# Gated cross-attention stack on one core: GpSimd in place of VectorE for the gate's normalised rows of ten batches

## The chip, the core and the metric

The kernel runs on one core of a Trainium2 chip, as one program with one launch. Its time is the device time of that core in microseconds. Three runs of the kernel before gave 856.76, 857.04 and 859.95 us; the median, 857.04 us, is what the forecast is set against.

The core has four compute engines with a queue of instructions each: TensorE (PE in the profile: matrix products and transposes), VectorE (DVE), ScalarE (ACT) and GpSimd (POOL). SyncE (SP) starts DMAs. Engines wait for each other through semaphores only; each engine works its queue strictly in the order in which the code wrote it.

## The reference

A stack of four gated layers on `x` (8 batches of 256 rows of width 256), with a context of 8 x 120 rows. Each layer is a cross-attention and a feed-forward part, both on normalised rows and both added through `tanh` of a gate:

```python
x = x + jnp.tanh(g_xattn[0]) * _L0_xattn_ref(_layernorm(x, axis=-1), ctx_1024, ctx_1024, ...)
x = x + jnp.tanh(g_ffn[0]) * _L0_ffn_ref(_layernorm(x, axis=-1), L0_ffn_gate, ...)
...
x = x + jnp.tanh(g_xattn[3]) * _L3_xattn_ref(ctx_1024, ctx_1024, _layernorm(x, axis=-1), ...)
x = x + jnp.tanh(g_ffn[3]) * _L3_ffn_ref(_layernorm(x, axis=-1), L3_ffn_wg, L3_ffn_w1, L3_ffn_w2)
```

with

```python
def _layernorm(x, axis=-1, eps=1e-05):
    m = jnp.mean(x, axis=axis, keepdims=True)
    v = jnp.var(x, axis=axis, keepdims=True)
    return (x - m) / jnp.sqrt(v + eps)
```

The first layer (0) and the last (3) have an attention with one head and a feed-forward part with experts. In both the experts' gate is a product of the normalised rows with a 256 x 8 matrix: in layer 0 each expert takes its 256 best tokens (`top_k` over the softmax) and a shared hidden layer works on all tokens; in layer 3 each token goes to its best expert, up to a capacity of 256. Layers 1 and 2 have attention with 16 heads, a spectral and a ternary feed-forward part; the change doesn't touch them.

## The kernel before, in words

All of `x` stays in SBUF, as 16 tiles of 128 rows x 256, two tiles a batch. The program goes: weights folded; **layer 0's attention and gate**, batch by batch (about 15 to 80 us); the shared hidden layer with the search for each expert's tokens beside it; the first experts; the two many-head layers as one stream; **layer 3's attention and gate** (about 670 to 740 us); the last experts.

The two bold stages are the same code, `one_gate(L)`, written once for each engine, with `L` 0 or 3. Each is a loop over steps `s`. A step works on several batches at once: the attention of batch `s` begins, the attention of batch `s-1` ends, and the gate of batch `s-2` is computed. Nothing but the order of the calls in each engine's loop sets the order of the work. The order of one step `s`:

- VectorE: `stats(one, s+1, 0)`, the mean and variance of the next batch for its attention (`bn_stats` L1745, `bn_aggr` L1748, plus epsilon L1750); `normalize(gt, s-2, 1, z2)`, the **gate's normalised rows** (L1760, two instructions, one a tile); `shift(s)`, the scores' maximum (L1773); `take_logits(s-3)` (L1791); `normalize(one, s+1, 0, z)`, the attention's normalised rows (L1760 too); `add_output(s-1)` (L1778, L1780, and L1784, which adds the attention's product to `x`); `take_values(s+1)` (L1768); `stats(gt, s-1, 1)`, the statistics for the gate, of rows that now hold the attention's result. In layer 3 there is routing work between these from step 5 on (L1801 to L1836).
- GpSimd: `rstd_of(one, s+1, 0)`, variance to the power -0.5 for the attention of the next batch (L456), then `rstd_of(gt, s-1, 1)`, the same for the gate. From step 7 of layer 3 it also starts the DMAs that move routed rows (L448).
- TensorE: `turn_z(s)` (transposes, L772), `turn_p(s-1)` (L802), `keys_values(s+1)`, `scores(s)`, `gate_turn(s-2)`, the **transposes of the gate's rows** (L823), then `values(s-1)`, the attention's product that `add_output` waits for, and `logits(s-2)`. All products have the line of the helper `mm`, L676. Before some of the transposes there are products without use (`FILL`: six before the first gate batch of layer 0, six before the sixth of layer 3).
- ScalarE copies transposes out of PSUM (L1414) and does the exponentials (L1466).
- SP stores the gate's rows of layer 0 to DRAM (L333), each after the semaphore `gate_z`, because the experts gather them from there later. In its queue the loads of the shared layer's weights (L338) stand behind the fourth of these stores.

The gate's rows go to `z2` in layer 0 (four tiles, used in turn) and to `zx` in layer 3 (a place for every tile). In the profile both are parts of one SBUF buffer, `arena`; the statistics and the powers lie in `small`. The semaphores by their names in the order of instructions: `one_var`, `one_rstd`, `one_z`, `one_y_ps` for the attention, `gate_var`, `gate_rstd`, `gate_z`, `gate_zT_ps` for the gate: statistics made, power made, rows made, and (`zT_ps`) rows transposed; `gate_stored0` and `gate_stored1` count landed stores; `one_y_ps` is the product in `values`.

Of the kernel before, what the change touches and what calls it, by code (L numbers as in the profile page):

```python
# [5 lines left out]
ALU = mybir.AluOpType  # L6
# [8 lines left out]
D = 256  # L15
KC = D // P
NB, SQ, SK = 8, 256, 120
T = NB * SQ
NT = T // P
TB = SQ // P  # L20
# [8 lines left out]
FILL = {0: {0: 6}, 3: {5: 6}}  # L29
GROUPS = [(0, 3), (3, 5), (5, 7), (7, 8)]  # L30
EARLY = 2 * GROUPS[0][1]
EPS = 1e-5
NEG = -1e30
BITS = 32
# [23 lines left out]
def flamingo_kernel(nc, d, out):  # L58
    ctx = ExitStack()
    with ctx:  # L60
# [7 lines left out]
        x = sb("x", [P, NT, D], F32)  # L68
# [52 lines left out]
        z = c.take(4 * D, "p (t n) -> p t n", t=4)  # L121
        zT = c.take(2 * KC * SQ, "p (u k n) -> p u k n", u=2, k=KC)
        z2 = c.take(4 * D, "p (t n) -> p t n", t=4)
# [54 lines left out]
        zx = c.take(NT * XROW, "p (t n) -> p t n", t=NT)  # L178
# [9 lines left out]
        c.at = after_common + 2 * KC * CAP + 2 * MC * CAP + 2 * TB * D  # L188
        late = c.take((NT - 2 - EARLY) * CAP, "p (i n) -> p i n", i=NT - 2 - EARLY)
        assert c.at <= 14272  # L190
# [38 lines left out]
        mv = c.take(8, "p (t n) -> p t n", t=4)  # L229
        ve = c.take(4)  # L230
        rstd = c.take(4)
# [63 lines left out]
        gt = sems("gate", f"{ln_names} l_ps l_sb stored0 stored1 picked prob rank_ps rank_sb slot moved")  # L295
# [139 lines left out]
        def _(g):  # L435
# [15 lines left out]
            def one_gate(L):  # L451
                b0 = NB * (L // 3)

                def rstd_of(q, k, a):
                    g.wait_ge(q["var"], b0 + k + 1)
                    g.tensor_tensor(rstd[:, 2 * a:2 * a + 2], ve[:, 2 * a:2 * a + 2], mhalf[:, 0:2], ALU.pow).then_inc(q["rstd"], 1)  # L456

                if L == 0:
                    rstd_of(one, 0, 0)
                for s in range(NB + 1):  # L460
                    if s + 1 < NB:
                        rstd_of(one, s + 1, 0)
                    if L == 3 and s in (7, 8):
                        if s == 7:
                            g.wait_ge(ex["blank"], 16)
                            g.wait_ge(gt["slot"], 1)
                        for t in range(3 * (s - 7), 3 * (s - 6)):
                            move(t)
                    if 1 <= s:
                        rstd_of(gt, s - 1, 1)  # L470
                if L == 3:
                    g.wait_ge(ex["rows0"], 16)
                    for n, (a, b) in enumerate(GROUPS[1:]):
                        g.wait_ge(gt["slot"], 5 if b == NB else n + 2)
                        for t in range(2 * a, 2 * b):
                            move(t)
# [1250 lines left out]
        def _(v):  # L1727
# [12 lines left out]
            def one_gate(L):  # L1740
                b0 = NB * (L // 3)
# [69 lines left out]
                def take_ranks(n):  # L1811
                    w = 2 * (GROUPS[n][1] - GROUPS[n][0])
                    o = psum[4][:, 256:256 + w * E].rearrange("p (t e) -> p t e", t=w)
                    v.wait_ge(gt["rank_ps"], n + 1)
                    V.tensor_scalar(o8[:, 0:w, :], o, float(CAP), float(2 * T), ALU.is_gt, ALU.mult)
                    V.tensor_tensor(a8[:, 0:w, :], o, bcast(base8, 1, w), ALU.add).then_inc(gt["rank_sb"], 1)
# [27 lines left out]
                def main():  # L1844
# [19 lines left out]
                    for s in range(NB + 3):  # L1864
# [4 lines left out]
                        if L == 3 and s == NB + 1:  # L1869
                            take_logits(s - 3)  # L1870
                            pick_expert(2)
                        if 2 <= s < NB + 2:
                            normalize(gt, s - 2, 1, z2)
                        if s < NB and (L or s):
                            shift(s)
# [14 lines left out]
                            take_values(s + 1)  # L1890
                        if L == 3 and s == 6:
                            take_ranks(0)
                        if 1 <= s <= NB:
                            stats(gt, s - 1, 1)
                        if L == 3 and s == 6:
# [224 lines left out]
            def stream():  # L2120
# [69 lines left out]
                def side_stats(j):  # L2190
# [6 lines left out]
                    v.drain()  # L2197
                    V.tensor_scalar(veS, mv[:, 2:4, 1], EPS, None, ALU.add).then_inc(f1["var"], 1)

# [193 lines left out]
```

## Time and profile before

| | us |
|---|---|
| median of three runs | 857.04 |
| the three runs | 856.76, 857.04, 859.95 |
| span of the profiled execution | 859.9 |
| time of that execution (the run that stands for it) | 859.95 |
| TensorE busy | 829.8 (96% of the span), clock granted 0.993 of 2.4 GHz on average |
| VectorE busy | 459.7 (53%) |
| ScalarE busy | 332.7 (39%) |
| GpSimd busy | 227.6 (26%) |

How to read it: a share of the span is a mean over stages that are limited in different ways. The two stages of `one_gate` together last about 125 us; VectorE is busy for 80 to 90% of most of that time, and for almost nothing in the expert stages. The span and the time of the profiled execution differ by less than 0.1 us, so what lies around the span can be left out of account.

### The profile page before, as it was taken

What the parts mean: (1) busy time and instruction counts of PE and PEld (TensorE: products, weight loads), DVE (VectorE), ACT (ScalarE), POOL (GpSimd) and SP (SyncE); (2) the same over time, 40 slices, a digit from 0 to 9 for tenths busy, and PEclk for the clock granted to TensorE, in tenths of its full rate; (3) what the DMA queues carried; (4) which work ended last, traced back from release to release, by engine and by line L of the source; (5) the groups of instructions that cost most, each with busy time, mean ns of one, the idle gap of its engine ahead of it and who ended that gap; (6) DMA issues with size and microseconds to landing.
All of it is one profiled execution on the core that took longest, in us unless ns stands there. A gap on an engine that the chain in (4) does not pass through costs nothing.

```text
span 859.9 us, 15359 instructions
## 1 busy us (share of the span) xinstructions
PE 829.8 (96%) x5870; PEld 645.0 (75%) x5870; DVE 459.7 (53%) x1245; ACT 332.7 (39%) x642; POOL 227.6 (26%) x304
## 2 busy tenths in 40 slices
PE   8999999999999998899999999988999998999996
PEld 7875665678888886667777777755777777888885
DVE  3773775500132318677777777764999787100000
ACT  3344112112313224556455545646554444321211
POOL 1211333020425221001001301213788124421212
PEclk9998999999999999999999999999999999999999
DMA  7141911015746439000000000000000012454541
GB/s 247 26 147 41 351 29 52 26 44 208 238 134 229 117 79 339 2 2 2 2 1 2 2 2 2 2 1 2 1 1 2 26 38 87 149 191 140 188 138 23
DMA packets 35427, 71.14 MB, mean 83 GB/s; under 512 B 10642, under 2 KB 25370, under 8 KB 30491
## 3 DMA queue, kind: packets, MB, share of 16 engines
q1 hardware_dynamic: 28489, 60.46, 19.8%
q0 software_dynamic: 6144, 8.31, 5.0%
q10 hardware_dynamic: 722, 1.39, 0.4%
q8 instruction: 47, 0.77, 0.4%
q14 instruction: 25, 0.20, 0.1%
HBM read 55.50 MB, written 14.80 MB: 82 GB/s over the span
## 4 chain that ended last, share of the span: by engine, by line
PE 84%; DVE 8%; DVEq 2%; issue 2%; ACT 1%; DMA 1%; POOL 1%; POOLq 0%; SPq 0%; ACTq 0%
PE banks L676 76%; DVE small L2166 2%; PE banks L1223 2%; PE banks L1305 1%; PE banks L823 1%; PE banks L1237 1%; PE banks L1040 1%; ACT arena L1632 1%; DVE arena L1760 1%; PE banks L1261 1%; PE banks L1114 1%; DVEq L2167 0%; DVE small L1745 0%; PE banks L772 0%; DMA x<-acc 0%
## 5 line engine op out<-in xcount | busy, mean ns | idle before, releaser
L676 PE MATMUL banks<-arena 32*120 32x256 f32 (+6 forms) x1848 | 167.5, 375 | 7.4 <-DVE small L2166 4.2
L1414 ACT ACTIVATE arena<-banks 128x512 f32<-128x512 f32 (+4 forms) x183 | 105.7, 597 | 156.9 <-PE banks L823 34.1
L676 PEld LDWEIGHTS banks<-arena 32*120 32x120 f32 (+5 forms) x1848 | 105.6, 162 | 37.7 <-issue 16.1
L676 PE MATMUL banks<-ffw,arena 128*128 128x256 f32 (+2 forms) x640 | 117.3, 338 | 0.2 <-DVE x L1738 0.2
L676 PE MATMUL banks<-arena,ew 128*128 128x256 f32 x512 | 113.2, 380 | 0.7 <-ACT arena L1414 0.7
L676 PE MATMUL banks<-ew,arena 128*128 128x256 f32 x512 | 113.3, 380 | 0.0
L676 PEld LDWEIGHTS banks<-arena,ew 128*128 128x128 f32 x512 | 97.4, 190 | 14.1 <-ACT arena L1414 1.1
L676 PEld LDWEIGHTS banks<-ew,arena 128*128 128x128 f32 x512 | 96.4, 190 | 12.3
L676 PEld LDWEIGHTS banks<-ffw,arena 128*128 128x128 f16 (+1 forms) x640 | 84.5, 135 | 24.3 <-issue 3.0
L2166 DVE TENSOR_REDUCE small<-banks 128x16 f32<-128x1920 f32 x32 | 69.0, 2157 | 19.1 <-PE banks L676 18.9
L1632 ACT ACTIVATE arena<-banks,mcol 120x2048 f32<-120x2048 f32 x32 | 63.1, 1973 | 16.2 <-PE banks L676 16.2
L2113 DVE TENSOR_SCALAR arena<-banks,arena 128x256 f32<-128x256 f32 x16 | 7.1, 480 | 110.3 <-PE banks L676 110.3
L578 POOL TENSOR_TENSOR small<-small,mhalf 128x2 f32<-128x2 f32 x16 | 11.1, 692 | 195.6 <-DVE small L2137 195.6
L676 PE MATMUL banks<-arena,ffw 128*128 128x512 f32 x128 | 60.2, 615 | 0.0
L1573 ACT ACTIVATE arena<-banks,b1T 128x256 f32<-128x256 f32 x64 | 26.8, 470 | 77.0 <-PE banks L676 77.0
L1444 ACT ACTIVATE arena<-banks,b1T 128x512 f32<-128x512 f32 x32 | 21.9, 687 | 76.9 <-PE banks L676 76.9
L1575 ACT ACTIVATE arena<-banks 128x256 f32<-128x256 f32 x64 | 21.1, 381 | 78.1 <-PE banks L676 78.1
L456 POOL TENSOR_TENSOR small<-small,mhalf 128x2 f32<-128x2 f32 x31 | 22.6, 730 | 95.8 <-DVE small L1750 95.8
L2082 DVE TENSOR_SCALAR small<-arena,tg 128x2 f32<-128x2 f32 x8 | 1.8, 228 | 82.6 <-PE banks L676 82.6
L543 POOL DMA_INDIRECT arena<-zrow,small x16 | 17.8, 1114 | 101.4 <-DVE arena L2095 55.0
L533 POOL DMA_INDIRECT out<-arena x14 | 21.8, 1559 | 80.4 <-DVE arena L2113 64.8
L596 POOL TENSOR_TENSOR arena<-arena 128x256 f32<-128x256 f32 x64 | 38.8, 638 | 10.0 <-ACT arena L1659 9.9
(258 smaller groups left out, 1252.5 us busy)
## 6 DMA issues: line engine op xcount, KB each, us to landing
ew<-in_w SPq DMA_DIRECT2D x32, 1024.0 KB, 7.2
xrow<-arena SPq DMA_DIRECT2D x1, 2064.0 KB, 22.1
zrow<-arena SPq DMA_DIRECT2D x8, 256.0 KB, 2.2
ffw<-in_shared SPq DMA_DIRECT2D x2, 1024.0 KB, 6.9
acc<-x SPq DMA_DIRECT2D x4, 512.0 KB, 3.6
ffw<-in_tern SPq DMA_DIRECT2D x2, 1024.0 KB, 7.9
out<-x SPq DMA_DIRECT2D x8, 256.0 KB, 2.0
arena<-xrow SPq DMA_DIRECT2D x7, 258.0 KB, 4.1
```

Of the source, the lines that this page charges most:

```text
L456: g.tensor_tensor(rstd[:, 2 * a:2 * a + 2], ve[:, 2 * a:2 * a + 2], mhalf[:, 0:2], ALU.pow).then_inc(q["rstd"], 1)
L533: g.indirect_dma_start(to, bass.IndirectOffsetOnAxis(ap=at(e, j), axis=0), eout[:, e % 2, j, :], None, compute_op=ALU.add, **kw).then_inc( ...
L543: g.indirect_dma_start(G[:, u, j, 0:ROW], None, zrow, bass.IndirectOffsetOnAxis(ap=idx[:, TB * e + j:TB * e + j + 1], axis=0))\
L596: m = g.tensor_tensor(hw[:, t % 2, a:a + 256], h2[:, t % 2, a:a + 256], wrow[:, a:a + 256], ALU.mult)
L676: return pe.matmul(o, l, r, start=a, stop=b)
L1223: m = pe.transpose(OW[:, 512 * t + g_ * P:512 * t + (g_ + 1) * P], OP[:, g_, t * P:(t + 1) * P], ident[:, :])
L1414: return nc.scalar.activation(o, i_, ACT.Copy)
L1444: nc.scalar.activation(hT[:, m_, :], psum[m_ % 4][:, :], ACT.Gelu_apprx_tanh, bias=b1T[:, E * MC + m_:E * MC + m_ + 1]).then_inc(sh["h_sb" ...
L1573: m = nc.scalar.activation(heT[:, u, m_, :], src, ACT.Gelu_apprx_tanh, bias=b1T[:, n * MC + m_:n * MC + m_ + 1])
L1575: m = nc.scalar.activation(heT[:, u, m_, :], src, ACT.Relu)
L1632: nc.scalar.activation(PT[0:SK, c].rearrange("p h n -> p (h n)"), SC[0:SK, :], ACT.Exp, bias=mcol[0:SK, L - 1, k:k + 1]).then_inc(q["p_exp ...
L2166: V.tensor_reduce(nmx[:, t, :], s, AX.X, ALU.max, negate=True).then_inc(q["max"], 1)
```

## The change

GpSimd computes the gate's normalised rows for the first six batches of layer 0 and the first four of layer 3; VectorE does the rest as before. The new function `gate_rows(k)` stands in GpSimd's loop between the two powers of a step. It waits for GpSimd's own earlier instructions (`drain`), in layer 0 from the third batch on also for the transposes and the store that free its tiles, and raises the same semaphore as before. VectorE, which overwrites the mean and the statistics of the gate with the next batch's, now waits for that semaphore before it does so.

```diff
@@ -29,6 +29,7 @@
 EARLY = 2 * GROUPS[0][1]
+POOLED = {0: 6, 3: 4}
@@ -455,11 +456,25 @@
+                def gate_rows(k):
+
+                    g.drain()
+                    if k >= 2 and L == 0:
+                        g.wait_ge(gt["zT_ps"], k - 1)
+                        g.wait_ge(gt[f"stored{k % 2}"], 16 * (k // 2))
+                    for t in range(TB):
+                        dst = zx[:, 2 * k + t, 0:D] if L == 3 else z2[:, 2 * (k % 2) + t, :]
+                        m = g.tensor_scalar(dst, x[:, 2 * k + t, :], mv[:, 2 + t, 0:1], rstd[:, 2 + t:3 + t],
+                                            ALU.subtract, ALU.mult)
+                    m.then_inc(gt["z"], 1)
+
                 if L == 0:
                     rstd_of(one, 0, 0)
                 for s in range(NB + 1):
                     if s + 1 < NB:
                         rstd_of(one, s + 1, 0)
+                    if 2 <= s < 2 + POOLED[L]:
+                        gate_rows(s - 2)
@@ -1869,7 +1884,7 @@
-                        if 2 <= s < NB + 2:
+                        if 2 + POOLED[L] <= s < NB + 2:
                             normalize(gt, s - 2, 1, z2)
@@ -1890,6 +1905,8 @@
+                        if 2 <= s <= 1 + POOLED[L]:
+                            v.wait_ge(gt["z"], b0 + s - 1)
                         if 1 <= s <= NB:
                             stats(gt, s - 1, 1)
```

GpSimd's instructions in layer 0, from the first gate batch on, before the change:

```order
L456 TENSOR_TENSOR small<-small,mhalf 128x2 [waits gate_var]
L456 TENSOR_TENSOR small<-small,mhalf 128x2 [waits one_var]
L456 TENSOR_TENSOR small<-small,mhalf 128x2 [waits gate_var]
L456 TENSOR_TENSOR small<-small,mhalf 128x2 [waits one_var]
L456 TENSOR_TENSOR small<-small,mhalf 128x2 [waits gate_var]
```

and the same stretch of the changed program (its lines are numbered some 15 higher):

```order
L457 TENSOR_TENSOR small<-small,mhalf 128x2 [waits gate_var]
L457 TENSOR_TENSOR small<-small,mhalf 128x2 [waits one_var]
L467 TENSOR_SCALAR arena<-x,small 128x256 x2
L457 TENSOR_TENSOR small<-small,mhalf 128x2 [waits gate_var]
L457 TENSOR_TENSOR small<-small,mhalf 128x2 [waits one_var]
L467 TENSOR_SCALAR arena<-x,small 128x256 x2
L457 TENSOR_TENSOR small<-small,mhalf 128x2 [waits gate_var]
```

Each pair of row instructions stands behind the power that waits for the attention's statistics of the next batch, and in front of the next power for the gate.

VectorE's instructions of step 3 in layer 0, from the next batch's statistics on, before the change:

```order
L1745 BN_STATS small<-x 128x6 x2
L1748 BN_AGGR small<-small 128x2 x2
L1750 TENSOR_SCALAR small<-small 128x2
L1760 TENSOR_SCALAR arena<-x,small 128x256 [waits gate_rstd]
L1760 TENSOR_SCALAR arena<-x,small 128x256
L1773 TENSOR_REDUCE small<-banks 128x2 [waits one_s_ps]
L1791 COPY small<-banks 128x16 [waits gate_l_ps]
L1760 TENSOR_SCALAR arena<-x,small 128x256 [waits one_zT_ps,one_rstd]
L1760 TENSOR_SCALAR arena<-x,small 128x256
```

and in the changed program, up to the gate's statistics:

```order
L1760 BN_STATS small<-x 128x6 x2
L1763 BN_AGGR small<-small 128x2 x2
L1765 TENSOR_SCALAR small<-small 128x2
L1788 TENSOR_REDUCE small<-banks 128x2 [waits one_s_ps]
L1806 COPY small<-banks 128x16 [waits gate_l_ps]
L1775 TENSOR_SCALAR arena<-x,small 128x256 [waits one_zT_ps,one_rstd]
L1775 TENSOR_SCALAR arena<-x,small 128x256
L1793 RECIPROCAL small<-small 128x2 [waits one_p_sb]
L1795 TENSOR_SCALAR small<-small,tg 128x2
L1799 SCALAR_TENSOR_TENSOR x<-banks,small,x 128x256 [waits one_y_ps]
L1799 SCALAR_TENSOR_TENSOR x<-banks,small,x 128x256
L1783 TENSOR_TENSOR arena<-banks,rows 120x256 [waits one_y_ps,one_KT_sb]
L1760 BN_STATS small<-x 128x6 [waits gate_z]
```

The gate's pair is gone from between the statistics and the maximum; the statistics for the gate wait for `gate_z`. TensorE's and SP's instructions and their waits are the same in both.

## Rows read from the trace of the kernel before

**Rows 1.** The page's chain that ended last, by engine, over the whole span.
```profile
PE 84%; DVE 8%; DVEq 2%; issue 2%; ACT 1%; DMA 1%; POOL 1%; POOLq 0%; SPq 0%; ACTq 0%
```

**Rows 2.** TensorE's waits, whole span: total us, times, longest us.
```profile
PE banks L823 <- DVE arena L1760: 4.2, 6, 1.6
```

**Rows 3.** Timeline, TensorE, first layer: start us, us, instructions, [idle before <- releaser].
```profile
30.12 0.60 PE L823 MATMUL banks<-ident,arena 128*128 128x128 f32 x4
...
43.05 0.63 PE L823 MATMUL banks<-ident,arena 128*128 128x128 f32 x4
...
49.40 0.60 PE L823 MATMUL banks<-ident,arena 128*128 128x128 f32 x4
...
55.95 0.63 PE L823 MATMUL banks<-ident,arena 128*128 128x128 f32 x4
...
61.89 1.04 PE L823 MATMUL banks<-ident,arena 128*128 128x128 f32 x4 [0.62 <-DVE arena L1760]
...
68.99 3.47 PE L676 MATMUL banks<-arena,ffw 128*128 128x512 f32 x4
```

**Rows 4.** Timeline, VectorE, first layer.
```profile
44.62 0.88 DVE L1784 SCALAR_TENSOR_TENSOR x<-banks,small,x 128x256 f32<-128x256 f32 x2
...
47.21 0.74 DVE L1745 BATCH_NORM_STATS2 small<-x 128x6 f32<-128x256 f32 x2
...
48.49 0.73 DVE L1760 TENSOR_SCALAR arena<-x,small 128x256 f32<-128x256 f32 x2
...
64.67 0.88 DVE L1784 SCALAR_TENSOR_TENSOR x<-banks,small,x 128x256 f32<-128x256 f32 x2 [2.16 <-PE banks L676]
...
72.33 0.94 DVE L1760 TENSOR_SCALAR arena<-x,small 128x256 f32<-128x256 f32 x2 [0.80 <-POOL small L456]
```

**Rows 5.** Timeline, GpSimd, first layer.
```profile
29.40 0.78 POOL L456 TENSOR_TENSOR small<-small,mhalf 128x2 f32<-128x2 f32 x1 [0.91 <-DVE small L1750]
...
48.60 0.85 POOL L456 TENSOR_TENSOR small<-small,mhalf 128x2 f32<-128x2 f32 x1 [0.53 <-DVE small L1750]
...
60.28 0.69 POOL L456 TENSOR_TENSOR small<-small,mhalf 128x2 f32<-128x2 f32 x1 [4.26 <-DVE small L1750]
...
72.62 0.97 POOL L483 TENSOR_SCALAR rows<-rows,tg 128x256 f32<-128x256 f32 x1
```

**Rows 6.** Timeline, TensorE, last layer: the gate's transposes of batches 1, 4 and 5.
```profile
683.25 0.66 PE L823 MATMUL banks<-ident,arena 128*128 128x128 f32 x4 [1.09 <-DVE arena L1760]
...
701.99 0.63 PE L823 MATMUL banks<-ident,arena 128*128 128x128 f32 x4
...
709.68 0.63 PE L823 MATMUL banks<-ident,arena 128*128 128x128 f32 x4 [1.57 <-DVE arena L1760]
```

**Rows 7.** Timeline, GpSimd, two instructions with a drain between them.
```profile
663.94 0.22 POOL L601 TENSOR_SCALAR small<-small 128x1 f32<-128x1 f32 x1
664.31 0.56 POOL L603 TENSOR_TENSOR small<-small,mhalf 128x1 f32<-128x1 f32 x1
```

**Rows 8.** Groups by line and shape, GpSimd: busy us, mean ns, idle before.
```profile
L508 POOL TENSOR_SCALAR rows<-rows,tg 128x256 f32<-128x256 f32 x3 | 2.8, 936 | 4.0 <-DVE small L1945 4.0
...
L513 POOL TENSOR_SCALAR arena<-arena 8x120 f32<-8x120 uint8 x1 | 0.6, 622 | 0.1
```

**Rows 9.** Timeline, GpSimd, last layer: power for the attention's fourth batch.
```profile
682.63 0.78 POOL L456 TENSOR_TENSOR small<-small,mhalf 128x2 f32<-128x2 f32 x1 [0.53 <-DVE small L1750]
```

**Rows 10.** Timeline, SP's queue, first layer: the loads of the shared weights.
```profile
49.66 0.95 SPq L338 DMA_DIRECT2D ffw<-in_shared  x2
```

**Rows 11.** Windows: us, PE, PEld, DVE, ACT, POOL busy (x), PEclk, DMA share, GB/s.
```profile
60.00:62.00 2.00, 1.38 (x10) 1.11 (x10) 1.16 (x5) 0.00 (x0) 0.69 (x1) 0.99 0.00 0
62.00:64.00 2.00, 2.00 (x7) 1.73 (x7) 0.44 (x4) 1.03 (x4) 0.00 (x0) 0.50 0.38 131
...
72.00:74.00 2.00, 2.00 (x8) 1.01 (x7) 0.94 (x2) 1.04 (x2) 1.59 (x3) 0.95 0.00 0
...
708.00:710.00 2.00, 0.43 (x5) 0.35 (x4) 1.85 (x10) 0.00 (x0) 0.78 (x1) 1.00 0.00 0
```

## The prediction

> **What bounds the kernel now.** I read the chain of waits first, then TensorE's waits, then the two stages that the change touches, engine by engine. The chain lies on TensorE for 84% of the span and on VectorE for 8% [rows 1], so anything that keeps TensorE waiting is paid in full, and anything that only relieves VectorE is paid back only where TensorE waits for it. TensorE's own list says where that is: before the gate's transposes (L823) it waits for the normalised rows (L1760) six times, 4.2 us in all [rows 2]. That 4.2 us is the most that faster rows could give.
>
> In the first layer the gate's transposes follow each other evenly: the first is at 30.12, the fifth at 55.95, so a step takes 25.83 / 4 = 6.46 us, and none of these has a wait in front [rows 3]. A step is one loop of four links. (a) From the gate's transposes, TensorE's product and VectorE's addition (L1784) start 44.62 - 43.05 = 1.57 us later. (b) VectorE then does the addition, takes the values, makes the gate's statistics and comes to the next batch's statistics at 47.21: 2.59 us later [rows 3, 4]. (c) GpSimd starts the power (L456) on those at 48.60, 1.39 us later [rows 5]. (d) VectorE meanwhile writes the gate's rows at 48.49, in 0.73 us [rows 4], and the next transposes go at once. In the last layer the same loop takes (701.99 - 683.25) / 3 = 6.25 us [rows 6].
>
> **The change, part by part.** VectorE loses ten pairs of L1760, 0.73 us each, 7.3 us in all. I cost this relief at nothing: in the loop above the pair is replaced by something longer, and the relief behind it only makes VectorE wait earlier for the product that comes after the gate's transposes. The wait for the rows that VectorE gets before the gate's statistics costs nothing either, because those stand behind the addition, which already waits for a product that TensorE makes after it has turned the rows.
>
> The rows move to GpSimd, and the order of GpSimd's instructions decides when they come: the power for the attention's next batch stands in front of them. They can't start when the statistics of the gate are ready, but only after (c). So a step's rows now need, from the start of that power:
> - the power, 0.69 us: it takes 0.78 and 0.85 where VectorE's pair runs beside it and 0.69 where it doesn't [rows 5], and that pair is gone;
> - the drain, 0.15 us: a GpSimd instruction that ends at 663.94 + 0.22 has its successor behind a drain at 664.31 [rows 7];
> - the two instructions. No row of before has this form (128x256, two operations, both with a column of scalars). The nearest below is the same shape with one operation, 936 ns [rows 8] (the single one at 72.62 took 0.97 [rows 5]). The nearest above has two operations on 120 elements, 622 ns [rows 8], which scaled by 256/120 is 1.33 us. I take 1.0, near the same shape, since the upper one contains a fixed part and a conversion from bytes. The pair is 2.0 us, with ends 1.87 and 2.65;
> - 0.18 us from the rows to the transposes, as between VectorE's rows (48.49 + 0.73) and the transposes at 49.40 [rows 3, 4].
>
> Together 3.02 us from the power's start. Link by link the loop becomes 1.57 + 2.59 + 1.39 + 3.02 = 8.57 us.
>
> First layer, six batches. The first batch: its power starts at 29.40 [rows 5], rows are usable at 32.42 where TensorE began at 30.12: +2.3. Four loops: 4 x (8.57 - 6.46) = +8.4. The sixth batch has no attention batch in front of it: the power of its own statistics starts at 60.28 [rows 5], 4.33 us after the fifth transposes (55.95), and 4.33 + 3.02 = 7.35 replaces 61.89 - 55.95 = 5.94 [rows 3]: +1.4. Sum +12.1 us.
>
> Last layer, four batches. The first: 682.63 [rows 9] + 3.02 = 685.65 against 683.25 [rows 6]: +2.4. Three loops: 3 x (8.57 - 6.25) = +7.0. The fifth batch is written by VectorE again, and its chain from the fourth transposes, 709.68 - 701.99, is VectorE's [rows 6]: no change. Sum +9.4 us.
>
> The stores of the gate's rows wait on the same semaphore and move with them. SP's queue has the load of the shared weights behind the fourth store: it goes out at 49.66 [rows 10]; and no DMA is busy any more from 60 us on [rows 11], so it takes 10 us at most. It would go some 8.6 us later (2.3 + 3 x 2.11) and be there by 69; TensorE uses it first at 68.99 + 12.1 = 81.1 [rows 3]. Hidden, with 12 us to spare. The wait for that store before the third and later batches asks for one two steps back, two loops of 6.46 us and more earlier. Also hidden.
>
> So far +21.5 us with TensorE at its full clock. The clock is the second term. The granted clock went from 1.00 (2.4 GHz) to 0.50 (1.2 GHz) at 62 us, after a stretch in which TensorE had been busy 1.38 of 2 us, and was back by 72 to 74 us [rows 11]. In the last layer it stayed at 1.00 through a stretch with 0.43 of 2 us busy [rows 11], with a wait of 1.57 us in front of the transposes [rows 6]. Idle spells that are now 0.6 to 1.6 us long and rare become about 2.1 us in every step, longer than any that these rows show. At the low clock link (a) took 64.67 - 61.89 = 2.78 instead of 1.57 us [rows 3, 4]: +1.21 in each step whose transposes fall into it; the rest of TensorE's work has the step's slack. I count it for five steps of the first layer, where a smaller spell was enough, and two of the last: 7 x 1.21 = +8.5 us. Bounds: none, or all of TensorE's work (below).
>
> Sum: 12.1 + 9.4 + 8.5 = **+30.0 us**. The profiled execution spans 859.9 us and is the highest of the three runs; against the median of 857.04 the forecast is **887.0 us**.
>
> On GpSimd's neighbours: beside a GpSimd multiplication, VectorE's pair took 0.94 instead of 0.73 us [rows 4, 5]; a power beside it took up to 0.85 instead of 0.69. So the two slow each other by 0.1 to 0.2 us, and I add nothing. The Trainium skill (SBUF — State Buffer, section "Who interferes with whom") says more: such VectorE instructions and GpSimd share a pair of ports, held by one for its whole instruction while the other is fully blocked. The sum by it is the second rival's. The rows at 72.33 and 72.62 speak against it: VectorE's second instruction ended at 73.27, inside GpSimd's 72.62 to 73.59.
>
> **The rivals.**
> - *The clock holds.* No idle spell of the last layer lowered it [rows 6, 11]. Then 857.0 + 21.5 = 878.5 us; with the pair at its ends (10 x -0.13, 10 x +0.65) 877 to 885. 27%.
> - *The rows are held up by VectorE.* GpSimd's pair now runs beside VectorE's remaining pair for the attention (0.73 us) in nine of ten steps (the sixth batch has none). If one fully stops the other, the rows come up to 0.73 later: +6.6 on the forecast, 893.6 us. For it: the power's 0.85 beside the pair, against it 72.33. The port rule above is this case. 10%.
> - *The clock stays low through both stages.* TensorE's own step is then what lasts: 6.46 x 2.78 / 1.57 = 11.4 instead of 8.57, eight times, on top of 878.5: +23, 901 us. Against it: it was back ten us after the fall. 8%.
> - *GpSimd is as fast as VectorE* on this form: the pair 0.73 instead of 2.0, 1.27 less in ten batches, and with less waiting the clock holds: 878.5 - 12.7 = 866 us. Its rows of 936 ns for one operation speak against it. 7%.
> - *Not slower:* the freed VectorE gives TensorE its waits back. The place is the last layer, where VectorE is level with TensorE; the prize is a part of the 4.2 us [rows 2], so 855 to 857 us. It decides by one point: the rows must be usable within 2.19 us of the start of VectorE's statistics, as at present (49.40 - 47.21 [rows 3, 4]). GpSimd's power alone ends at 1.39 + 0.69 = 2.08. It would take rows that get in front of that power, and GpSimd's order has them behind it. That the change wouldn't do what it says can be excluded in the same way: the order shows ten pairs on GpSimd. 4%.
>
> **How the numbers follow.** The forecast, 44%: 887.0, its own range 880 to 894 (three to ten steps at the low clock, and the pair's upper end). The range is 869 to 899: it leaves out the last two rivals and the low clock throughout, 19%, and takes in the rest. 0.5% of this kernel is 4.3 us, about what a measurement can tell from no change. Slower by more: all but the last rival, 95%, as even the fast-GpSimd case is 8 us up. Same 3%, faster 2%.
>
> **What would show it.** In the profile after: ten pairs of TENSOR_SCALAR 128x256 on GpSimd, about 1.0 us each, starting 0.8 to 0.9 us after the power's start; L823's waits now released by GpSimd, near 2 us in each of ten steps, some 20 us in all; transposes 8.5 us apart in both layers (9.7 where the clock is low); GpSimd some 20 us busier, VectorE 7.3 us less; more stretches at a granted clock of 0.5 before 80 us and around 685 to 715 us; everything between the stages just shifted by some 12 to 18 us. Wrong it is if the transposes stay 6.5 us apart, if the GpSimd pair takes well under 1.8 us, or if the distance from the power to the rows shows a start that isn't behind it.

## The result: 38 us slower, and the profile after

The changed kernel took 896.59 us in the median of four runs (893.86 to 899.76), the kernel before 858.50 us (856.76 to 861.50, four runs). The ratio is 1.0454, with a 95% interval of 1.0432 to 1.0475: slower by 38.1 us. The forecast was 887.0 us with a range of 869 to 899, so the sign and the place were right, and 9.6 us of the time were missed. The measured time lies above the 880 to 894 that the forecast gave to its own mechanism, near the upper end of the range.

Two things about the reference point. The kernel before runs in two ways: in one set of seven runs four took 856.67 to 856.86 us, at a mean clock of 0.997 to 0.999, and three took 861.56 to 861.80 at 0.992 to 0.993. And the time of a run is 1.7 to 2.1 us more than its span, in every run whose span is listed (861.74 with a span of 860.0; 893.86 with 891.8). The profiled execution of before, with its span of 859.9, was thus one of those at 861.7 us, 4.7 above the median, and not the one of 859.95 us as the table ahead of the prediction had it. The 4.9 us between the two ways fit the stretch at low clock after 62 us [rows 11]. No profile of a better execution of before is at hand, but e3 below has the same first layer without that stretch, and it is 4.8 us shorter. Below, "clean before" is the kernel before without that stretch (856.86 us).

The first lines of the page of the changed kernel, the row of the granted clock in 40 slices (22.3 us each), and the chain by engine:

```profile
span 891.8 us, 15369 instructions
...
PE 846.4 (95%) x5870; PEld 659.2 (74%) x5870; DVE 453.9 (51%) x1225; ACT 333.0 (37%) x642; POOL 252.6 (28%) x324
...
PEclk9876999999999999999999999999999779999999
...
PE 81%; DVE 8%; POOL 3%; DVEq 3%; issue 2%; ACT 2%; POOLq 1%; ACTq 0%
```

GpSimd is on the chain with 3% of the span, 27 us, where it had 1% [rows 1]. VectorE is 5.8 us less busy and gained nothing by it. The granted clock is below full in five slices, three of the first layer and two of the last. TensorE is "busier" by 16.6 us with the same 5870 instructions: no new work, but more of it at 1.2 instead of 2.4 GHz.

TensorE's waits in front of the gate's transposes (L823 before, L838 now):

```profile
PE banks L838 <- POOL arena L467: 16.0, 6, 4.2
...
PE banks L838 <- DVE arena L1775: 2.5, 3, 1.9
```

Six waits of 16.0 us for GpSimd stand where six of 4.2 us for VectorE stood [rows 2]; the four other steps with GpSimd's rows have none. The transposes themselves show why. They are, in the first layer and the last (start, time for four; the wait is in brackets), with the first large product of the shared layer and the transposes of the seventh batch (88.23):

```profile
32.44 0.80 PE L838 MATMUL banks<-ident,arena 128*128 128x128 f32 x4 [2.78 <-POOL arena L467]
...
42.42 0.63 PE L838 MATMUL banks<-ident,arena 128*128 128x128 f32 x4 [0.24 <-POOL arena L467]
...
51.49 0.63 PE L838 MATMUL banks<-ident,arena 128*128 128x128 f32 x4 [2.55 <-POOL arena L467]
...
61.91 1.06 PE L838 MATMUL banks<-ident,arena 128*128 128x128 f32 x4
...
71.90 1.09 PE L838 MATMUL banks<-ident,arena 128*128 128x128 f32 x4 [2.79 <-POOL arena L467]
...
81.11 1.09 PE L838 MATMUL banks<-ident,arena 128*128 128x128 f32 x4
...
86.52 1.88 PE L691 MATMUL banks<-arena,ffw 128*128 128x512 f32 x4
88.23 0.60 PE L838 MATMUL banks<-ident,arena 128*128 128x128 f32 x4
...
703.40 1.12 PE L838 MATMUL banks<-ident,arena 128*128 128x128 f32 x4 [4.15 <-POOL arena L467]
...
713.70 0.63 PE L838 MATMUL banks<-ident,arena 128*128 128x128 f32 x4
...
723.27 1.09 PE L838 MATMUL banks<-ident,arena 128*128 128x128 f32 x4 [3.45 <-POOL arena L467]
...
733.57 0.60 PE L838 MATMUL banks<-ident,arena 128*128 128x128 f32 x4
...
741.52 0.63 PE L838 MATMUL banks<-ident,arena 128*128 128x128 f32 x4 [1.85 <-DVE arena L1775]
```

The first four steps of the first layer take 9.98, 9.07, 10.42 and 9.99 us, where a step took 6.46, and the sixth batch comes 9.21 us after the fifth instead of 5.94 [rows 3]. In the last layer the steps take 10.30, 9.57 and 10.30, where they took 6.25 [rows 6]. The seventh batch's transposes came at 72.30 in before's profile; they are 15.9 us later now.

**One loop at full clock** is the second step, 42.42 to 51.49. GpSimd and VectorE in it:

```profile
38.97 0.69 POOL L457 TENSOR_TENSOR small<-small,mhalf 128x2 f32<-128x2 f32 x1 [0.49 <-DVE small L1765]
39.85 2.43 POOL L467 TENSOR_SCALAR arena<-x,small 128x256 f32<-128x256 f32 x2 [0.19 <-issue]
46.73 0.71 POOL L457 TENSOR_TENSOR small<-small,mhalf 128x2 f32<-128x2 f32 x1 [4.45 <-DVE small L1765]
47.94 0.69 POOL L457 TENSOR_TENSOR small<-small,mhalf 128x2 f32<-128x2 f32 x1 [0.50 <-DVE small L1765]
48.89 2.46 POOL L467 TENSOR_SCALAR arena<-x,small 128x256 f32<-128x256 f32 x2 [0.26 <-issue]
```

```profile
43.96 0.88 DVE L1799 SCALAR_TENSOR_TENSOR x<-banks,small,x 128x256 f32<-128x256 f32 x2 [0.22 <-PE banks L691]
...
49.38 0.88 DVE L1775 TENSOR_SCALAR arena<-x,small 128x256 f32<-128x256 f32 x2
```

The power at 46.73 is the gate's own; the rows could start 0.7 us later. They wait for the one at 47.94, the attention's, which VectorE's statistics release. Link by link: transposes at 42.42, addition at 43.96 (1.54 later; forecast 1.57), the attention's power at 47.94 (3.98; forecast 2.59 + 1.39 = 3.98), the power 0.69 (0.69), the drain 0.26 (0.15), the pair 2.46 (2.0), and 0.14 from 51.35 to the transposes at 51.49 (0.18). Every link but two is as forecast to 0.04 us. The loop is 9.07 instead of 8.57.

**Loops at low clock.** Two-microsecond windows of all engines (stretch, its length, then busy time of PE, PEld, DVE, ACT and POOL in us, granted clock as a share of 2.4 GHz, DMA share, GB/s):

```profile
40.00:42.00 2.00, 2.00 (x13) 1.35 (x11) 0.00 (x0) 0.61 (x2) 2.00 (x2) 1.00 0.02 4
...
58.00:60.00 2.00, 2.00 (x5) 0.80 (x3) 0.00 (x0) 0.61 (x2) 2.00 (x2) 0.50 0.00 0
60.00:62.00 2.00, 2.00 (x10) 1.94 (x10) 0.00 (x0) 0.00 (x0) 0.38 (x1) 0.50 0.35 118
...
720.00:722.00 2.00, 0.00 (x0) 0.00 (x0) 1.30 (x6) 0.00 (x0) 1.81 (x3) 1.00 0.00 0
...
724.00:726.00 2.00, 2.00 (x8) 1.64 (x6) 0.00 (x0) 1.28 (x5) 0.00 (x0) 0.50 0.00 0
```

TensorE stands idle while the rows are made (720 to 722 us: busy 0.00 us, clock still 1.00), and is at 1.2 GHz afterwards (724 to 726: 0.50) through the work of the step. It is back 6 to 13 us after the fall. It falls five times in the ten steps, about every second step: in or just behind each of the five waits of 2.55 to 4.15 us for GpSimd above, and not at the other five transposes, which had a wait of 0.24 us or none. At low clock the work of a step fills it: GpSimd's pair ended at 60.38, but the transposes came at 61.91, with no wait, since TensorE was still at work. That step took 10.42 us, and its bound was TensorE.

### The profile page after: what moved, and what is told of

It reads as the page before. It is cut to its first block, busy times and chain, and to the rows that moved or that the text cites. A ratio compares the mean times of both kernels' runs of the same rounds, so it can differ in the third digit from the quotient of the medians.

```text
span 891.8 us, 15369 instructions
## 1 busy us (share of the span) xinstructions
PE 846.4 (95%) x5870; PEld 659.2 (74%) x5870; DVE 453.9 (51%) x1225; ACT 333.0 (37%) x642; POOL 252.6 (28%) x324
## 3 DMA queue, kind: packets, MB, share of 16 engines
q10 hardware_dynamic: 722, 1.39, 0.4%
## 4 chain that ended last, share of the span: by engine, by line
PE 81%; DVE 8%; POOL 3%; DVEq 3%; issue 2%; ACT 2%; POOLq 1%; ACTq 0%
PE banks L691 74%; DVE small L2183 2%; POOL arena L467 2%; PE banks L1238 2%; PE banks L838 1%; PE banks L1320 1%; PE banks L1252 1%; PE banks L1055 1%; ACT arena L1647 1%; PE banks L1276 1%; PE banks L1129 1%; POOL small L457 1%; DVE arena L1775 1%; DVE x L1799 1%; DVE small L1760 0%
## 5 line engine op out<-in xcount | busy, mean ns | idle before, releaser
L691 PE MATMUL banks<-arena 32*120 32x256 f32 (+6 forms) x1848 | 172.3, 378 | 7.4 <-DVE small L2183 4.1
L691 PEld LDWEIGHTS banks<-arena 32*120 32x120 f32 (+5 forms) x1848 | 109.1, 164 | 38.8 <-issue 16.6
L2183 DVE TENSOR_REDUCE small<-banks 128x16 f32<-128x1920 f32 x32 | 69.0, 2157 | 18.5 <-PE banks L691 18.3
L611 POOL TENSOR_TENSOR arena<-arena 128x256 f32<-128x256 f32 x64 | 39.0, 642 | 10.7 <-ACT arena L1674 10.5
```

The source lines that it names most:

```text
L611: m = g.tensor_tensor(hw[:, t % 2, a:a + 256], h2[:, t % 2, a:a + 256], wrow[:, a:a + 256], ALU.mult)
L691: return pe.matmul(o, l, r, start=a, stop=b)
L2183: V.tensor_reduce(nmx[:, t, :], s, AX.X, ALU.max, negate=True).then_inc(q["max"], 1)
```

## The experiments

Every experiment has its own runs of the kernel before, on the same chip as it. In the first set (e1 to e4) they have a median of 856.86 us over seven runs, in the last (e5) 856.93 over eleven. A set between (e7 to e10) was on a chip where the kernel before takes 866.34 us in the median of 29 runs; it is compared by ratios within the set, and by distances in the traces.

### e1: the clock held with products without use

```diff
-FILL = {0: {0: 6}, 3: {5: 6}}
+FILL = {0: {0: 16, 1: 10, 2: 10, 3: 10, 4: 10, 5: 8}, 3: {0: 14, 1: 10, 2: 10, 3: 10, 5: 6}}
```

> The changed kernel with products without use in front of the gate's transposes of the ten batches (8 to 16 of them, 0.225 us each at the full clock), so that TensorE works through most of its wait; nothing else differs. Theory A (the rows come late by GpSimd's chain, and the low clock is a second term): the granted clock stays at 1.0 in both stages, the transposes are 9.0 us apart in both layers (1.57 + 2.59 + 1.39 + 0.69 + 0.20 + 2.43 + 0.14), against 9.1 to 10.4 in the changed kernel, and the time falls by some 8 to 14 us to 883 to 889. Rival B (the low clock is only a sign of the waiting and costs nothing): the time stays at 896 within 3 us. Rival C (the products get in the way): slower than 896.

Measured 886.96 us (884.90 to 888.76), ratio 1.0325 [1.0276, 1.0373]; the changed kernel has 1.0454. The mean clock is 0.992 to 0.998 instead of 0.963 to 0.970. The gate's transposes in the first layer, with the seventh batch's, and two of the last layer:

```profile
32.38 0.66 PE L838 MATMUL banks<-ident,arena 128*128 128x128 f32 x4 [0.55 <-POOL arena L467]
...
41.36 0.65 PE L838 MATMUL banks<-ident,arena 128*128 128x128 f32 x4
...
68.36 0.66 PE L838 MATMUL banks<-ident,arena 128*128 128x128 f32 x4 [0.22 <-POOL arena L467]
...
76.21 0.66 PE L838 MATMUL banks<-ident,arena 128*128 128x128 f32 x4 [0.71 <-POOL arena L467]
...
82.04 0.60 PE L838 MATMUL banks<-ident,arena 128*128 128x128 f32 x4
...
732.31 0.98 PE L838 MATMUL banks<-ident,arena 128*128 128x128 f32 x4 [1.57 <-DVE arena L1775]
...
742.99 0.60 PE L838 MATMUL banks<-ident,arena 128*128 128x128 f32 x4
```

The steps of the first layer are all 9.0 us long ((68.36 - 32.38) / 4), the pure loop. The clock's share of the loss is 896.59 - 886.96 = 9.6 us between medians, and 11.6 us against the two runs of 884.9 and 885.2 that kept the clock nearly throughout. In the profiled run it still fell behind the wait of 1.57 us at 732.31, and the next transposes came 10.68 us later, where 7.0 is usual [rows 6]: that is the 3.7 us between its kinds of runs. What is left, 28 us, is the longer loop, and 1.2 us between the two stages that are counted below. Rivals B (the low clock costs nothing, 896 us) and C (the products get in the way) are thus wrong.

### e2 and e3: one layer at a time

```diff
-POOLED = {0: 6, 3: 4}
+POOLED = {0: 6, 3: 0}
```

> GpSimd makes the rows in the first layer alone (six batches, none in the last). The two traces give the first layer 16 to 17 us of the loss. Theory A: the parts add up, so 858.5 + 17 = 875 us, 873 to 879. Rival (one stage's delay moves or hides the other, by the clock or by a transfer): the two single-layer runs do not add up to the 38 us of the change.

and `{0: 0, 3: 4}`:

> GpSimd makes the rows in the last layer alone (four batches). The two traces give the last layer 14 to 15 us. Theory A: 858.5 + 15 to 20 = 873 to 879 us, and with the first-layer run the gains over before add up to 38 within 4 us. Rival as there.

Measured: the first layer alone 883.63 us (875.12 to 884.16), ratio 1.0261 [1.0194, 1.0328]; the last alone 870.91 (869.19 to 872.12), ratio 1.0144 [1.0099, 1.0189]. Against 856.86 these are +26.8 and +14.1, together +40.8, where the whole change makes +39.7 against the same 856.86 (+38.1 against the 858.50 of its own runs of before). The two add up, within their intervals; neither pays for or hides the other. Each alone missed what I expected of it: the first layer costs more (873 to 879 us expected), the last less (873 to 879 us again, where the traces alone had given it 14 to 15 us). In the first, part of that is a stage at low clock that reached further (its first large product came at 90.37, against 86.52 with the whole change), and one of its four runs, at 875.12 and a clock of 0.986, did without.

The trace of e3 also gives what was missing in before's: a first layer on VectorE whose clock holds.

```profile
29.96 0.60 PE L838 MATMUL banks<-ident,arena 128*128 128x128 f32 x4
...
55.79 0.63 PE L838 MATMUL banks<-ident,arena 128*128 128x128 f32 x4
61.72 0.63 PE L838 MATMUL banks<-ident,arena 128*128 128x128 f32 x4 [0.62 <-DVE arena L1775]
...
67.52 0.60 PE L838 MATMUL banks<-ident,arena 128*128 128x128 f32 x4
```

The seventh batch stands at 67.52, 4.8 us before the 72.30 of before's profile. This is the "clean before" against which the first layer is counted below.

### e4: the rows ahead of the attention's power

```diff
                 for s in range(NB + 1):
-                    if s + 1 < NB:
-                        rstd_of(one, s + 1, 0)
                     if 2 <= s < 2 + POOLED[L]:
                         gate_rows(s - 2)
+                    if s + 1 < NB:
+                        rstd_of(one, s + 1, 0)
```

> The changed kernel with GpSimd's two calls in the other order: the gate's rows before the power for the attention's next batch. Theory A (each step's loop is as long as its links): the rows start 0.20 us after the gate's own power, the loop is 4.16 + 0.86 + 0.20 + 2.43 + 0.14 = 7.8 instead of 9.0 us at the full clock, still above the 6.46 and 6.25 of before: with waits of about 1.5 us and a clock that falls in some steps 873 to 883 us. Rival B (the place in GpSimd's queue is not what delays the rows; the duration alone is): no gain, 893 to 900. Rival C: the attention's rows, whose power now comes later, become the wait (L787 transposes), and it stays above 885.

Measured 887.87 us (886.37 to 890.66), ratio 1.0352 [1.0303, 1.0400]. Steps at full clock take 8.07 and 8.04 us instead of 9.07. But the clock still fell:

```profile
38.71 0.63 PE L838 MATMUL banks<-ident,arena 128*128 128x128 f32 x4 [1.47 <-POOL arena L467]
...
46.75 1.09 PE L838 MATMUL banks<-ident,arena 128*128 128x128 f32 x4 [1.53 <-POOL arena L467]
...
58.71 1.06 PE L838 MATMUL banks<-ident,arena 128*128 128x128 f32 x4
```

One step, 46.75 to 58.71, took 11.96 us. TensorE worked through almost all of it at 1.2 GHz (granted clock 0.50 in every window from 48 to 60 us), so TensorE itself was the bound there. The order is worth 896.59 - 887.87 = 8.7 us of the 38, less than I expected (873 to 883 us), and this run doesn't tell how much of it is loop and how much clock. It lies above 885 as in rival C, but not by C's mechanism: in front of the attention's transposes (L787) TensorE waits 0.8 us in three waits, exactly as in the changed kernel. What lengthens it is the clock.

### e5: the same, with the clock held

The edit of e4 and, fewer than in e1 since the loop is shorter,

```diff
-FILL = {0: {0: 6}, 3: {5: 6}}
+FILL = {0: {0: 11, 1: 6, 2: 6, 3: 6, 4: 6, 5: 8}, 3: {0: 10, 1: 6, 2: 6, 3: 6, 5: 6}}
```

> The rows are made ahead of the power, as in e4_rows_first, and TensorE's wait is covered with useless products, as in e1_fill, but with fewer of them, since the loop is shorter: only the length of the loop at full clock is left of the change. Theory A (the loop and the clock are two separate costs): the clock holds, the gate's transposes stand 8.05 us apart in the first layer (e4_rows_first had 8.04 to 8.07 where its clock was full, e1_fill 9.0) and about as much in the last, so the kernel lies about ten steps x 0.95 us = 9 to 10 us below e1_fill: a ratio of 1.020 to 1.024 to its own kernel before. Theory B (the 8.7 us that e4_rows_first gained came mainly from a clock that was low for less time): with the clock held in both, the order is worth 3 to 5 us: a ratio of 1.027 to 1.030. TensorE should wait under 3 us in all for GpSimd's rows.

Measured 876.44 us (875.62 to 879.48, six runs), ratio 1.0220 [1.0193, 1.0246]: 10.5 us below e1, as theory A has it, and outside the 1.027 to 1.030 of theory B. Loop and clock are two separate costs; TensorE waits 2.3 us in all for GpSimd. Inside the loop, from the transposes at 46.92 to those at 54.96:

```profile
46.83 0.71 POOL L457 TENSOR_TENSOR small<-small,mhalf 128x2 f32<-128x2 f32 x1
51.53 0.69 POOL L457 TENSOR_TENSOR small<-small,mhalf 128x2 f32<-128x2 f32 x1 [3.99 <-DVE small L1765]
52.48 2.42 POOL L467 TENSOR_SCALAR arena<-x,small 128x256 f32<-128x256 f32 x2 [0.25 <-issue]
```

```profile
47.58 0.73 DVE L1775 TENSOR_SCALAR arena<-x,small 128x256 f32<-128x256 f32 x2 [1.63 <-POOL small L457]
...
48.77 0.88 DVE L1799 SCALAR_TENSOR_TENSOR x<-banks,small,x 128x256 f32<-128x256 f32 x2
```

The rows now start behind the gate's own power (51.53), which saves the 1.2 us between the two powers. But the attention's power comes late in its turn (46.83, behind the pair), VectorE waits 1.63 us for it, and the addition begins 1.85 us after the transposes instead of 1.54. So 0.3 us are given back, and the loop is 8.04, not 7.8. Whichever of the two goes first on GpSimd, the other one's reader waits. The +19.5 us that remain are mainly the price of the duration: the pair takes 2.42 us where VectorE writes the same rows in 0.73, and ten times the 1.69 us between them are 16.9 us. The drain, the 0.3 us given back and what lies between the stages are in the rest; no run takes them apart.

### e10: GpSimd's instruction with one operation

e1's idea with a pair that subtracts the mean only: this kernel leaves out the multiplication of the gate's rows of the ten batches by the power, and with it the column of scalars that it reads, so its result is not the reference's. The products without use are 8 a step.

```diff
-                        m = g.tensor_scalar(dst, x[:, 2 * k + t, :], mv[:, 2 + t, 0:1], rstd[:, 2 + t:3 + t],
-                                            ALU.subtract, ALU.mult)
+                        m = g.tensor_scalar(dst, x[:, 2 * k + t, :], mv[:, 2 + t, 0:1], None, ALU.subtract)
```

> The run with products in front of the transposes (e1), with GpSimd's two instructions doing one operation instead of two: the rows are x minus the mean and are not multiplied by the power, so the gate works on rows that are not scaled; fewer products (8 instead of 10) fit the shorter wait. Theory A (the form's duration goes into every step in full): 2 x 0.94 instead of 2 x 1.22 us, transposes 8.4 instead of 9.0 us apart, ten batches x 0.56 = 5.6 us less than e1's 887: 881. Rival (GpSimd's time per instruction doesn't depend on the second operation, the 1.22 us come from its column of scalars or from VectorE's neighbourhood): transposes 9.0 us apart, 887.

Measured 886.54 us (885.97 to 888.33) on the slower chip, ratio 1.0228 [1.0181, 1.0275]. Here is the group of GpSimd's instructions, in the changed kernel and then in e10 (count, busy us, mean ns; the mean holds the pairs that VectorE slowed, so it is above the 1.22 us of an undisturbed one):

```profile
L467 POOL TENSOR_SCALAR arena<-x,small 128x256 f32<-128x256 f32 x20 | 25.4, 1276 | 2.2 <-issue 2.2
```

```profile
L467 POOL TENSOR_SCALAR arena<-x,small 128x256 f32<-128x256 f32 x20 | 18.9, 954 | 2.1 <-issue 2.1
```

and one pair of e10 in the order of time:

```profile
37.91 1.86 POOL L467 TENSOR_SCALAR arena<-x,small 128x256 f32<-128x256 f32 x2 [0.19 <-issue]
```

The pair is 1.86 instead of 2.43, and the gate's transposes of the first layer stand 8.4 us apart instead of 9.0, as theory A has it; the rival (9.0) is wrong. The second operation costs 0.29 us an instruction, and 0.6 us of each loop. Ten loops make 6 us of it. Whether the operation itself costs this or the second column of scalars that goes with it, this edit can't tell, since it takes both away. The ratios of e1 and e10 are further apart, 0.97% or 8 us. The chips differ and a low stretch like that of e1 after 732 us is absent here, so I take the 6 us of the distances and leave the rest open.

### e7, e8 and e9: the kernel before, alone

e9 puts VectorE's new wait into the kernel before, with nothing moved:

```diff
+                        if 2 <= s <= 1 + {0: 6, 3: 4}[L]:
+                            v.wait_ge(gt["z"], b0 + s - 1)
                         if 1 <= s <= NB:
                             stats(gt, s - 1, 1)
```

> The kernel before with VectorE's new wait alone (the rows stay on VectorE, which waits for its own semaphore before the gate's statistics, in ten steps). Theory: costs nothing, 857 within 1 us for the undisturbed kind of run, as I costed it. Rival: VectorE stops at it each time, up to 0.2 us in ten steps, 2 us.

865.71 us (ten runs), ratio 0.9997 [0.9971, 1.0023]. The wait costs nothing, as the prediction had it. Here `gate_z` is raised by VectorE itself, so this shows that the wait as an instruction is free; that it doesn't hold VectorE up when GpSimd raises it is seen in the loop above, where the addition comes 1.54 us after the transposes.

e7 adds three products without use before the sixth batch of the first layer of before (`FILL = {0: {0: 6, 5: 3}, 3: {5: 6}}`), where its clock sometimes falls:

> The kernel before with three products without use in front of the gate's transposes of the sixth batch of the first layer (0.7 us, TensorE waits 0.6 us there). The kernel before has runs of two kinds, 856.7 and 861.7 us, with a mean clock of 0.998 and 0.992. Theory A (the low stretch from 62 to 72 us is worth the 5 us between them, and the waits before it cause it): all runs near 857, the mean clock 0.998 in all, no run at 861.7. Rival (what decides is not TensorE's waits): both kinds of run remain, or the products only add 0.1 to 0.7 us.

e8 is e7 with the routing work of step 5 of the last layer (`pick_expert(0)`), which delays VectorE's rows of the fifth batch, moved behind the rows of step 6:

```diff
                             normalize(gt, s - 2, 1, z2)
+                        if L == 3 and s == 6:
+                            pick_expert(0)
...
-                        if L == 3 and s in (5, 7, 10):
-                            pick_expert((5, 7, 10).index(s) + (s == 10))
+                        if L == 3 and s in (7, 10):
+                            pick_expert((7, 10).index(s) * 2 + 1)
```

> The kernel before with the three products of the run above, and in the last layer the first group's choice of experts (five small VectorE instructions, 1.3 us) moved from the end of step 5 to behind the gate's rows of step 6. TensorE waited 1.57 us in front of the fifth batch's transposes for rows that stood behind them. Theory A: that wait goes, some of it comes back at the ranks or the next transposes (0.57 us): 0.5 to 1.5 us faster than the run above, 855.5 to 856.5. Rival: the wait moves to the next step in full, no difference.

e7: 866.46 us (twelve runs), ratio 0.9991 [0.9969, 1.0013]. e8: 864.93 (twelve runs), ratio 0.9984 [0.9962, 1.0006]. Neither can be told from no change, and on this chip neither the kernel before nor e7 has the two clearly separate kinds of runs on which e7's theory rested, so that theory stays untested. In e7's profile the first layer has no low stretch, but neither has e9's, which waits its 0.62 us there without extra products; so this doesn't show that the products removed it. One stands in the last layer, behind a wait that the profile of before has too [rows 6]:

```profile
704.59 1.09 PE L823 MATMUL banks<-ident,arena 128*128 128x128 f32 x4 [1.57 <-DVE arena L1760]
...
712.88 0.66 PE L823 MATMUL banks<-ident,arena 128*128 128x128 f32 x4 [0.27 <-DVE arena L1760]
```

```profile
704.00:706.00 2.00, 1.42 (x6) 1.36 (x7) 1.78 (x8) 0.29 (x1) 0.66 (x1) 0.64 0.00 0
706.00:708.00 2.00, 2.00 (x13) 1.54 (x12) 0.58 (x2) 1.13 (x6) 0.00 (x0) 0.51 0.00 0
```

e8 took that wait away (the fifth transposes followed after 6.22 us, with none), but in front of L802 TensorE now waits 1.3 us for another piece of VectorE's work, where before has 0.4. So nothing here beats the kernel before by more than the measurement can tell.

## Why the prediction was right, and what it mis-sized

Counted at full clock, the sum can be checked term by term: e1 against the clean before (e3's first layer), and for the last layer against before's own trace [rows 6].

| term | forecast | measured |
|---|---|---|
| first batch, first layer | +2.3 | 32.38 - 29.96 = +2.4 |
| four loops | +8.4 | (68.36 - 32.38) - (55.79 - 29.96) = +10.2 |
| sixth batch | +1.4 | (76.21 - 68.36) - (61.72 - 55.79) = +1.9 |
| seventh batch | 0 | (82.04 - 76.21) - (67.52 - 61.72) = 0.0 |
| last layer, first batch | +2.4 | +3.1 |
| three loops | +7.0 | (724.59 - 697.13) - (701.99 - 683.25) = +8.7 |
| fifth batch | 0 | (732.31 - 724.59) - (709.68 - 701.99) = 0.0 |
| the clock | +8.5 | +9.6 to +11.6 |
| between the stages | 0 | +1.2 |
| sum | +30.0 | +37.1 to +39.1 |

(The first batch of the last layer is counted from the last transposes of the many-head layers, which start at 664.9 in before and 675.7 in e1: 697.13 - 675.7 = 21.4 against 683.25 - 664.9 = 18.3.) The 1.2 us between the two stages are in the traces of the changed kernel, e1 and e2, all with the first layer's rows on GpSimd, and 0.9 of them are two waits of TensorE for an addition of VectorE in the ternary part (L1753): 0.82 us at 629.25 and 0.34 at 674.30 in the changed kernel, where before has a single one of 0.22. The changed work isn't there; why VectorE comes later there stays open. The measured sum is to be set against the clean before: 896.59 - 856.86 = +39.7, and +38.1 against the median of the four runs.

- **The order of GpSimd's queue** was the step on which the size rested, and it holds: the pair stands behind the attention's power in every loop. The chain "transposes, addition, statistics, power" was forecast link by link to 0.04 us.
- **The duration of the pair** is the term that was mis-sized. I took 2.0 us, near the same shape with one operation [rows 8]; it is 2.43, and 2.60 to 2.73 where VectorE works beside it at the start. The right reading was that a second operation, with its column of scalars, isn't free on GpSimd: 936 ns for one, 1.22 us for two. The row with two operations on 120 elements [rows 8] scaled to 1.33 us and was nearer. In e1 the ten pairs take 25.5 us instead of 20 and the ten drains 2.2 instead of 1.5. Against that stand 0.13 us less in each of ten steps from the rows to the transposes (0.05 instead of 0.18, behind the products without use), and the earlier start in the next point. What is left of it is nearly all of the 4.8 us between 26.3 for the two stages as measured and 21.5 as forecast.
- **The first batch** (+2.3 forecast, +2.4 measured) agrees by luck. GpSimd's power started at 28.71 in e1, where e3 has 29.24, ahead by as much already at the power at 16 us (16.26 against 16.80), before any moved row; and the pair took 2.72 instead of 2.0. From the power to the transposes it is 3.67 us against 0.72 in e3, +2.95.
- **The clock** was forecast at seven steps of 1.21 us, five in the first layer and two in the last. That it would fall was right, and e1 shows it as a cost of its own. Step by step, the changed kernel's trace against e1's gives 6.1 us in the first layer (first to seventh batch, 55.8 us against 49.7) and 2.9 in the last (first to fifth, 38.1 against 35.2), in seven steps of 1.0 to 1.4 us, five and two; the three others differ by 0.1 to 0.2. The count came out, but partly by luck, since the form was not as told: the clock falls about every second step, and three of the steps whose work runs at 1.2 GHz (10.42, 10.30 and 10.30 us, no wait at their end) are bounded by TensorE itself instead of the loop with one longer link. The rival in which the clock is low throughout had that bound, at 11.4 us, but for all steps; the one step that ran low from end to end, in e4, took 11.96. The rival in which it holds had 878.5; held by force, it gives 887.
- **The relief of VectorE, its new wait and the stores** cost and bring nothing, as stated. VectorE is 5.8 us less busy, and TensorE waits for it before the fifth batch of the last layer as it did (1.85 us, before 1.57). The load of the shared weights went out at 60.80 instead of 49.66 [rows 10], was there by 70, and its reader came at 86.52. (The prediction reads from [rows 11] that no DMA is busy from 60 us on; the row of 62 to 64 us shows a share of 0.38. The row of 60 to 62 shows none, so the load was over by then and the conclusion stands.)
- **The two engines side by side.** GpSimd's pair takes 2.43 us alone, and more where VectorE's pair (29.50, 0.73 us) overlaps its start:

```profile
29.67 2.72 POOL L467 TENSOR_SCALAR arena<-x,small 128x256 f32<-128x256 f32 x2 [0.20 <-issue]
```

  The other way round, VectorE's pair at 49.38 (above) began 0.49 us after GpSimd's at 48.89, whose first instruction lasts 1.2 us, and took 0.88 instead of 0.73. So one slows the other by 0.15 to 0.3 us, and the rival in which the rows come 0.73 us later in each step is wrong. The Trainium skill (SBUF — State Buffer, "Who interferes with whom") has one of the two fully blocked while the other holds the shared ports for its instruction, when VectorE's instruction runs in a mode that uses both pairs of ports, which it says a `tensor_scalar` can. No row shows the mode of these. If it were that one, VectorE's pair could not have ended before 48.89 + 1.2 + 0.73 = 50.8; it ended at 50.26, and the measurement decides.
- **The point at which it would not have been slower** (rows usable within 2.19 us of the statistics) was out of reach even with the best order: in e5 the pair alone is longer than that.

## What to carry to other kernels

Before work goes from a busy engine to an idle one, follow the loop that it is a link of: here the link got 1.7 us longer (2.43 for 0.73) and moved behind another wait, and every step paid for both, while the relief of the busy engine was worth nothing because no one waited for it. Look at what stands ahead of the moved work in the queue of its new engine, and take its duration from a row with the same number of operations and columns of scalars, not only the same shape. And where TensorE waits more in each step, price the work after the wait at the low clock too: here a quarter of the loss or a little more was that, and useless products in the wait gave nearly all of it back.

## What the runs showed of the hardware that I had not expected

- GpSimd's TENSOR_SCALAR on 128x256 f32 takes 1.22 us with two operations and two columns of scalars, and 0.93 with one of each. VectorE's pair, with two operations, takes 0.73, so 0.37 for each.
- The clock's fall isn't set by the program alone. Of seven runs of the kernel before, unchanged, three have the time (4.9 us more) and the mean clock of the execution whose profile shows the low stretch after 62 us. A wait of 1.57 us in the last layer left the clock at 1.00 in before and in e9, and was followed by 0.50 in e7 and e1.
- The same program took 857 us on two chips and 866 on a third. In e7's and e9's traces from that one TensorE waits 4.5 and 5.9 us for VectorE's slot tables in the last layer (L1834), a wait that isn't in the list of the other chips; e8's stands idle 3.9 us at the same product, and e10's waits 1.8 us for those tables. The cause stays open.
